# A delta-rule layer on one core: the recurrence's first chunk without its zero state, and TensorE's loop cut at another place

## The reference

```python
q, k, v = silu(short_conv(x @ Wq.T)), silu(short_conv(x @ Wk.T)), silu(short_conv(x @ Wv.T))   # 4 taps each
beta = sigmoid(x @ Wb.T)
q, k = l2norm(q), l2norm(k);  v, kb = v * beta, k * beta
A = -(kb @ k.T), strictly lower;  T = inverse of (I - A);  u = T @ v;  w = T @ kb      # in each chunk
for chunk in chunks:                       # S starts at zero
    u_i = u - w @ S
    o   = q @ S + lower(q @ k.T) @ u_i
    S   = S + k.T @ u_i
paths = (short_fir(v), long_fir(v), o, v)
probs = floored softmax of a gelu MLP over (x, means and variances of the paths)
out   = rmsnorm(sum(probs * paths)) @ Wo.T
x = layernorm(x + out);  then top-2 of 8 experts by x @ router_w
```

## Time and profile before

| | |
|---|---|
| median of three runs | 2219.92 us |
| profiled execution | 2203.36 us |
| its span, first to last instruction | 2201.5 us |
| busy: PE, DVE, ACT, POOL | 70%, 65%, 39%, 27% of the span |
| mean granted clock of PE | 0.814 of full speed |

### The profile page before, as it was taken

How to read it: one execution, slowest core, us unless ns; L and a number is a source line. 1 busy time by engine, 2 the same in 40 slices (tenths; PEclk the granted TensorE clock), 3 DMA queues, 4 the chain that set the end, 5 groups by cost and what they waited for, 6 DMA issues and landing times. The chain is left out here.

```text
span 2201.5 us, 40915 instructions
## 1 busy us (share of the span) xinstructions
PE 1541.8 (70%) x12345; PEld 1172.0 (53%) x12346; DVE 1422.9 (65%) x3883; ACT 864.6 (39%) x1606; POOL 597.8 (27%) x504
## 2 busy tenths in 40 slices
PE   6872528869868868868768678688318999999600
PEld 3562217547556556456466376385206777777500
DVE  7992354786876867867858867864663444444376
ACT  6750412424523524524424434323224444444333
POOL 6770110120240330330420420512362333333200
PEclk9996756968959959959959869868559999999855
DMA  5657430131242241241341440432422222222396
GB/s 192 196 191 192 108 81 7 20 106 49 66 119 68 56 123 55 64 121 50 84 116 35 99 112 23 107 88 71 134 94 76 87 87 87 87 87 85 128 324 221
DMA packets 304923, 225.41 MB, mean 102 GB/s; under 512 B 181792, under 2 KB 272928, under 8 KB 304512
## 3 DMA queue, kind: packets, MB, share of 16 engines
q1 hardware_dynamic: 282816, 166.15, 27.8%
q0 software_dynamic: 15616, 44.62, 5.6%
q10 hardware_dynamic: 6336, 12.58, 1.7%
HBM read 131.47 MB, written 91.82 MB: 101 GB/s over the span
## 5 line engine op out<-in xcount | busy, mean ns | idle before, releaser
L1880 POOL DMA_INDIRECT y_d<-C_yb,C_dest x136 | 130.4, 959 | 302.6 <-ACT C_yb L1990 280.6
L1354 DVE SCALAR_TENSOR_TENSOR B_conv<-B_ps_x,B_cw,B_conv 128x511 f32<-128x511 f32 (+2 forms) x192 | 143.5, 748 | 98.0 <-ACT B_conv L1133 92.7
L422 POOL DMA_INDIRECT xs_d<-x,slot_u x128 | 133.4, 1042 | 123.3 <-DVE m_acc L1704 86.5
L681 POOL MEMSET B_s_bd<- 128x512 f32 x8 | 4.2, 523 | 526.0 <-PE B_ps_b L929 526.0
L2117 DVE TENSOR_TENSOR C_xt_low<-C_ps_x,C_xt_high 128x256 fp32r<-128x256 f32 x136 | 57.7, 424 | 137.2 <-ACT C_xt_high L1974 137.2
L985 PE MATMUL B_ps_x<-B_xg,B_w1x 128*128 128x512 f32 x256 | 131.1, 637 | 14.0 <-DMA B_xg<-xT 14.0
L1133 ACT ACTIVATE B_conv<-B_ps_x,B_cw 128x512 f32<-128x512 f32 x64 | 43.9, 685 | 229.7 <-PE B_ps_x L760 229.7
L2111 DVE TENSOR_TENSOR C_av<-C_sg,C_ps_g 128x256 f32<-128x256 f32 x136 | 57.3, 421 | 117.9 <-ACT C_sg L1984 117.9
L1914 PE MATMUL C_ps_g<-C_w_high,C_xt_high 128*128 x272 | 121.9, 448 | 0.5 <-issue 0.5
L876 PE MATMUL B_ps_b<-area 32*32 32x32 f32 x1024 | 29.2, 236 | 127.0 <-DMA area<-scr_xt 124.9
L1914 PE MATMUL C_ps_g<-C_w_low,C_xt_high 128*128 x272 | 108.3, 398 | 0.0
(11 more groups left out here) (321 smaller groups left out, 4547.2 us busy)
## 6 DMA issues: line engine op xcount, KB each, us to landing
C_xb<-xs_d SPq DMA_DIRECT2D x136, 132.0 KB, 2.1
area<-y_d ACTq DMA_DIRECT2D x12, 1024.0 KB, 5.4
A_band<-fir_long POOLq DMA_DIRECT2D x32, 256.0 KB, 7.0
A_work<-xT SPq DMA_DIRECT2D x16, 512.0 KB, 4.9
v_d<-A_v_tok SPq DMA_DIRECT2D x16, 512.0 KB, 3.4
short_d<-A_sh_tok SPq DMA_DIRECT2D x16, 512.0 KB, 3.2
B_xa<-xT SPq DMA_DIRECT2D x8, 1024.0 KB, 5.8
B_v_tok<-v_d SPq DMA_DIRECT2D x8, 1024.0 KB, 5.7
```

Of the source, the lines that this page charges most:

```text
L422: pool.indirect_dma_start(t["xs_d"][:, :], bass.IndirectOffsetOnAxis(ap=slot_u[:, c:c + 1], axis=0), x1[:, b, j, :], None).then_inc(done, 16)
L1354: V.scalar_tensor_tensor(conv[:, g % 2, k:], X[g % 2][:, :SEQ - k], cw[:, g // 4, gg % CH, 3 - k:4 - k], conv[:, g % 2, k:], ALU.mult, ALU ...
L1880: pool.indirect_dma_start(t["y_d"][:, :], bass.IndirectOffsetOnAxis(ap=dest[:, q:q + 1], axis=0), yb[:, u], None).then_inc(y_out[u], 16)
```

## The change

1. PE's first step of the recurrence loses both products with the state. The first residual is v times beta, which DVE forms in `first_rows`, between copies of the merging. POOL's `zero_state` and its semaphore go; `s_bd` is set to zero once, and the first update of a pair copies over the state's diagonal blocks in place of adding.
2. PE's loop now begins ahead of the merging: project(i+1, 0), betas(i+1), merges(i), solve_rows(i, 0), turn_mix(i-1), recur(i), and so on. The loops of DVE and ACT still begin at recur(i) and have one round less, their last two steps being written out.
3. With project(.., 0) go its group_a (ACT, behind the softmax's exponential) and taps (DVE, behind the first `weigh`). The projections and taps of each step of the recurrence are those that stood one step later. `z1` takes the memory of `z`, since `conv` is now in use at that time.
4. POOL's `mask_at` moves from ahead of the solver to between the halves of `mix_pool`, and waits for `x_back` too.
5. SP issues `load_xa` ahead of `solved_dmas`. PE turns the query norms after two of four `at_products`.

The core of the diff:

```diff
             def _(pool):
...
                 def mask_at(p):
                     pool.wait_ge(at_kept, 8 * (p + 1))
+                    pool.wait_ge(x_back, 128 * (p + 1))
...
                 def step(i, has_prev, has_next):
                     if has_next:
-                        zero_state(i + 1)
                         mask_blocks(i + 1)
-                        mask_at(i + 1)
                     if has_prev:
                         scatter(i - 1)
-                    for b in range(2):
-                        mix_pool(i, b)
+                    mix_pool(i, 0)
+                    if has_next:
+                        mask_at(i + 1)
+                    mix_pool(i, 1)
...
             def _(pe):
...
                 def betas(p):
                     need(pe, beta_ok, 2 * p)
+                    need(pe, rn_ok, 2 * p)
+                    if not isinstance(p, int) or p > 1:
+                        pe.wait_ge(sm_dve, 11 * (p - 2) + 1)
...
                 def recur(i, has_prev, has_next):
+                    if has_next:
+                        turn_betas(i + 1)
+                    to_state(i, 0)
+                    if has_next:
+                        project(i + 1, 1)
+                    within(i, 0)
+                    if has_prev:
+                        project_out(i - 1, 0)
+                        project_out(i - 1, 1)
+                    for s in range(1, TPB):
+                        from_state(i, s)
                         if has_next:
+                            project(i + 1, s + 1)
                         if has_prev and s == 3:
                             turn_x1(i - 1, 0)
+                        solve_rows(i, s)
+                        if has_next:
+                            select(i + 1, s - 1)
+                        if s < TPB - 1:
+                            to_state(i, s)
+                        elif has_next:
+                            select(i + 1, 3)
                         if has_prev and s == 3:
                             turn_x1(i - 1, 1)
+                        within(i, s)
...
                 def step(i, has_prev, has_next):
+                    if has_next:
+                        project(i + 1, 0)
+                        betas(i + 1)
+                    merges(i)
+                    solve_rows(i, 0)
+                    if has_prev:
+                        turn_mix(i - 1)
                     recur(i, has_prev, has_next)
...
-                    if has_next:
-                        merges(i + 1)
-                    turn_mix(i)
...
             def _(act):
...
                 def recur(i, has_prev, has_next):
+                    if has_next:
+                        tanh(i + 1)
+                    keep_u(i, 0)
+                    if has_prev:
+                        keep_o(i - 1)
+                    if has_next:
+                        group_b(i + 1, 0)
+                        group_a(i + 1, 1)
...
             def _(dve):
...
+                def first_rows(i):
+                    dve.wait_ge(v_in, 16 * (i + 1))
+                    V.tensor_tensor(r_sb[:], vv[:, :, 0], bb[:, :, 0, :].unsqueeze(3).to_broadcast([P, 2, HEADS, DH]),
+                                    ALU.mult).then_inc(r_r, 1)
...
                     softmax(i)
                     weigh(i, 0)
+                    if has_after:
+                        taps_of(i + 2, 0)
                     if has_next:
                         merge(i + 1, 0)
                     add_two(i, 0)
...
                     sum_squares(i, 1)
                     if has_next:
+                        first_rows(i + 1)
                         merge(i + 1, 4)
```

More of the change, by code:

```diff
@@ new lines, in to_state, with within @@
+                def to_state(i, s):
+                    pe.wait_ge(r_ub, 4 * i + s + 1)
+                    for c in range(4):
+                        b, m = c // 2, c % 2
+                        w = mm(B5[:, c * P:(c + 1) * P], k_tok[:, b * TPB + s, m * P:(m + 1) * P],
+                               u_sb[:, b, 2 * m:2 * m + 2, :], start=True, stop=True)
+                    w.then_inc(r_sx, 1)
+                def within(i, s):
+                    pe.wait_ge(r_ub, 4 * i + s + 1)
+                    if s == 0:
+                        pe.wait_ge(at_masked, i + 1)
+                    for c in range(8):
+                        b, h = c // 4, c % 4
+                        w = mm(B4[:, c * DH:(c + 1) * DH], at_t[:, b * TPB + s, h, :], u_sb[:, b, h, :],
+                               start=s == 0 and c == 0, stop=c == 7, skip_group_check=True)
+                    w.then_inc(r_o, 1)
@@ L1271, in merge_and_mix @@
                         merge(i + 1, 4)
-                    for k in range(4):
-                        b, m = k // 2, k % 2
-                        act.wait_ge(o_turned, 4 * i + k + 1)
-                        if k == 0:
-                            need(act, rt_mm, i)
-                        A(o_t[:, b, m, :], tails[m][:], ACT.Copy).then_inc(o_kept, 1)
                 def root_norm(i):
@@ L1515, in recur @@
                                         ALU.mult).then_inc(r_out, 1)
[L1516 to L1519 removed]
+                    for q in range(TPB):
+                        bn(q, 2)
+                    state(0)
+                    if has_next:
+                        taps_of(i + 1, 1)
+                    output(0)
+                    if has_prev:
+                        add_out(i - 1, 0)
+                        row_stats(i - 1, 0)
+                    dve.wait_ge(r_out, 4 * i + 1)
+                    bn(0, 3)
+                    residual(1)
+                    if has_next:
+                        taps_of(i + 1, 2)
+                    if has_prev:
+                        add_out(i - 1, 1)
+                        row_stats(i - 1, 1)
+                    state(1)
+                    for b in range(2):
+                        dve.wait_ge(sl_in[b], 16 * (1 + 2 * HEADS) * (i + 1))
+                    bn(0, 0)
+                    output(1)
+                    residual(2)
+                    if has_next:
+                        taps_of(i + 1, 3)
+                    if has_prev:
+                        scale_norm(i - 1)
+                    bn(0, 1)
+                    dve.wait_ge(r_out, 4 * i + 2)
+                    bn(1, 3)
+                    state(2)
+                    bn(1, 0)
+                    output(2)
+                    residual(3)
+                    if has_next:
+                        taps_of(i + 1, 4)
+                    bn(1, 1)
+                    dve.wait_ge(r_out, 4 * i + 3)
+                    bn(2, 3)
+                    for q in (2, 3):
+                        bn(q, 0)
+                        bn(q, 1)
+                    output(3)
+                    dve.wait_ge(r_out, 4 * i + 4)
+                    bn(3, 3).then_inc(st_dve, 1)
                 def stats(i):
@@ L1704, in place @@
                     V.tensor_tensor(m_acc[:], m_acc[:], m_sum[:], ALU.add).then_inc(rt, 1)
-                for g in range(4):
+                for g in range(5):
                     taps_of(0, g)
```

256 lines of the change are left out of this document (105 added, 151 removed).

## The result

The changed kernel takes 2189.56 us (median of four runs, 2174.8 to 2195.8), the kernel before, on the same chip, 2221.12 (2219.8 to 2223.7). The ratio is 0.985, with a 95% interval of 0.981 to 0.989: 31.6 us were won, where 56.4 were forecast, and 2189.56 lies above the forecast range (2155 to 2169) and the 8-in-10 range (2142 to 2185). The profiled execution took 2190.22 us. The four runs spread by 1%, those of before by 0.2%.

A forecast was written before the change was run, and what follows sets the result against it. It took PE's waits, in a loop of engines with one late at a time, to bound the kernel. Terms of 20 + 33 + 3 = 56 us off the 2219.9 median gave 2163 (2155 to 2169; 8-in-10 range 2142 to 2185).

The forecast's parts named there:

- the replay of the mixing: Between solver and merging: with the A^T mask between POOL's mixing halves, 2.3 of 3.6 us won per pair are left.
- My own sign of being wrong: Copies of the second merge step starting 26 us or more after the solver's end, against 22.6 before.
- I take the gain over as it is: Whole kernel: the 56.4 us worked out from the 2203.36 us profiled execution, taken off the runs' median of 2219.9.
- The first term: Ahead of the solver: moving the A^T mask ends a port block; 2.3 us in seven pairs, 3.8 in pair 0.
- The second and third term: Merging to second residual: loop edge and zero-state products go, 33 us in five pairs; 3 in pairs 1 and 7.
- DVE bounds the later steps: Later recurrence steps: DVE sets the pace, so key projections and taps shifted by one step change 0 us.
- Mask first: In the mixing, POOL's A^T mask gets the port ahead of DVE's waiting addition: price 10.5 us, 2174; chance 0.15.
- ACT late for u: Behind the merging, ACT's longer loop edge and second page stall make PE's transposes wait: 12 us, 2176; chance 0.15.
- The clock: Behind the merging, PE's clock stays low until the second residual: 13.5 us against 6.6 won, 2259; chance 0.03.
- The inverse not sooner: Ahead of the solver, masks on z come later behind the x load: 20 us of gain lost, 2183; chance 0.05.

The follow-up runs named there:

- split: Changed kernel with its scatter in two runs of 8 DMAs, the second after both gate halves' logits are kept: 2160.25 us, ratio 0.975.
- before, again: Kernel before, unedited, run and traced a second time as a control: 2215.87 us in its one run.

## Why the prediction was wrong

**The step that failed** is in the replay of the mixing: "Logits are ready at 936.7 and gain only about 0.4, so the softmax starts at 936.4 instead of 938.51", that is at +29.0. In the changed kernel the logits, not the solver, set when the softmax starts, because ACT's gelus stand still beside the scatter: it starts at +33.9 to +38.9 in pairs 2 to 7. What follows in the replay held. In pairs 2 to 6 of its two traces the softmax is at +33.8 to +38.9, and in nine of these ten the merge product follows it by 23.3 or 23.4 us (23.7 by the forecast), so the delay arrives whole. Before, 4.5 of 7.0 us were hidden under PE's wait for the inverse; the change used up that cover. My own sign of being wrong shows it: the copies of the second merge step start 32 us behind the solver's end, where I had named 26.

Stretches of the whole execution, from the timelines, against the first trace of before (us, minus is won):

| | forecast | changed | split | before, again |
|---|---|---|---|---|
| start to pair 2's masks on z | -8.1 | -13.1 | -15.1 | +1.9 |
| pairs 2 to 6: masks to merge product | -11.5 | +31.8 | +5.9 | +12.2 |
| pairs 2 to 6: on to second residual | -33 | -43.0 | -43.8 | -2.2 |
| pairs 2 to 6: on to the next masks | 0 | +12.7 | +14.7 | +4.4 |
| pair 7's masks to the end | -3.3 | -1.4 | -6.7 | -3.8 |
| sum | -56 | -13.0 | -45.0 | +12.5 |

Against the trace from which I forecast, 43 us are missing, and the row of the masks to the merge product alone misses 43.3; the others nearly cancel. Against before as it usually runs, with the stall, the split kernel gains 54 us (2214.4 to 2160.3), near the 56.4 forecast; but some 12 of them are the stall that before usually has and its first trace had not (last column), so that the agreement is in part luck. The stall costs the changed kernel at least 0.0066 of 2218 (its ratio of 0.982 against 0.975), some 15 us, since the split that takes it away has a price too; on the first chip, where 31.6 us were won, it is more.

**"I take the gain over as it is"** failed with it. The profiled execution was 16.6 us under the median of its kernel; I named that and didn't ask what it lacked. It lacked the stall.

**The first term, 20 us,** did not arrive, though its mechanism did. The solver starts at +3.9 instead of +8.1, of which the mask's move is 2.9 (+4.1 against +7.0 with the mask at its old place, both split). Where neither the stall nor the split stands in the way, with the scatter behind the mixing, the merge product is at +52.1, 2.9 sooner than in the first trace of before, where I kept 2.3. No kernel here has both this and a fast recurrence, so what the mask's move is worth in the whole is not shown; beside the split it is about 5.5 us.

**The second and third term, 36 us.** In pair 4 the stretch of 28.4 fell to 19.8, by 8.6, where I had worked out 7.3 and took 6.6; in pairs 2 to 6 it is 43.0 us in place of 33. Part of that is lost again behind the second residual, where I put 0 ("DVE bounds the later steps"): 12.7 us in five pairs against the first trace of before, 8.3 against the second. The masks on z of pair 2 also come 5 us sooner than forecast, before any scatter. The cause of either is not shown. The kernel with split scatter and the mask at its old place, which has neither the moved mask nor the stall, is 47.6 us under before; before has the stall, so this is not the two terms alone.

**The rivals.** Mask first: in the changed kernel's pair 4 DVE's addition went ahead of the mask, as in the replay, and the mask ahead of DVE's next weighing (947.31 and 948.36), which then took 4.84; with 23.3 us from softmax to merge product, where 23.7 were forecast, that rival's price was not paid. ACT late for u: no, it waited for PE (2.25). The clock: 0.50 through the merging, but 0.89 over 978 to 994, and the output projections took 1.9 each. The inverse not sooner: the solver began 1.2 us behind the mask. None of them was the cause, and I had no rival in which the gate is late.

## What to carry to other kernels

Before a forecast from one trace, ask why that execution is faster or slower than the median of its kernel; 0.7% can be a whole mechanism that the trace doesn't show. When a step ahead of a join of two chains is shortened, work out how late the other chain may be, in the worst execution and not only in the traced one. And look at what runs beside the path: here an unbroken run of 16 indirect DMAs from GpSimd held up engines that in the program don't wait for it, and a pause of 6 to 7 us in its middle was enough to keep the gelus even, though not the softmax.

## What the runs showed of the hardware

While POOL issues 16 indirect DMAs without a pause (one in 1.3 us), other engines start late or issue slowly: ACT stands still for up to 7.9 us in the gelus (in pair 4 of the changed kernel 7.12, all of it with the product there), PE goes down to one or two records in 1.4 us in the merging and DVE stands still, in part behind PE, for 8.7, with "issue" or "remote" ahead of them. It begins 4 to 15 us after the first of them and mostly lasts until 1 to 3 us behind the last. Two runs of 8 with 6 to 14 us between them did it only in small parts: the gelus are even, and with the shortest pause the softmax is up to 5 us late. One execution in two traces of the kernel before didn't have it at all.

That it is the supply of instructions is a guess. For it: PE, which waits for nobody in its merge product, slows too. By the Trainium skill (Runtime: NRT & Kernel Launch, "Instruction fetch mechanics") each engine fetches its instructions over a DMA queue of its own, which would allow it; the page takes this for hidden, which the trace would then contradict. Against the simplest form of it: moving ACT's text by 32, 112 or 251 instructions changed nothing. The DMA view, which shows packets of the instruction queues, doesn't decide. It has none from 957 to 973 in the kernel with the scatter behind the mixing and none from 912 to 932 in the changed one, but none from 976 to 996 in the changed one either, where no scatter runs. In the kernel before, the trace without the stall has none from 930 to 950, and the one with the stall has two at 932 to 936, amid its scatter. What tells executions with the stall from those without stays open, and so does how the scatter does it.
